# Re-placing four pieces of work in an attention and expert kernel: the maxima by couples, the late weight splits, gelu's table, and the last tokens' halves

## The reference, cut to what matters

```python
x = x + attention(layernorm(x), ctx)      # 8 heads of 64, softmax over the 1601 context rows
x = x + ffn(layernorm(x))                 # 1024 tokens

# attention: q = x Wq, k = ctx Wk, v = ctx Wv; softmax(q k^T / 8) v; then Wo and bo
# ffn: h = gelu(x w1 + b1) for a shared expert and for 8 experts,
#      expert_out = h w2 + b2, weighted by the router's two largest softmax probabilities,
#      plus the shared expert's output
```

## Time and profile before

| | us |
|---|---|
| median of 3 runs | 410.04 |
| profiled execution | 411.02 |
| its span, first to last instruction | 409.1 |
| PE busy | 399.1 (98%) |
| DVE busy | 284.6 (70%) |
| ACT busy | 247.9 (61%) |
| POOL busy | 237.0 (58%) |

### The profile page before, as it was taken

One profiled execution on the slowest core, in us unless ns is written; L12 is line 12 of the kernel. 1 busy time (PEld: TensorE's weight loads), 2 busy tenths in 40 slices (PEclk: granted clock), 3 DMA queues, 4 the chain that ended last, 5 costly groups with the idle time before them and its releaser, 6 DMA issues.

```text
span 409.1 us, 9721 instructions
## 1 busy us (share of the span) xinstructions
PE 399.1 (98%) x3718; PEld 333.0 (81%) x3718; DVE 284.6 (70%) x580; ACT 247.9 (61%) x399; POOL 237.0 (58%) x167
## 2 busy tenths in 40 slices
PE   8999999999999999999999999999999989999996
PEld 7787979798878887978788879797888777768886
DVE  4977788797537787976368778775586844566644
ACT  5677557383856472828555637287354554797882
POOL 7437668785804874729038756371183950687881
PEclk9999999999999999999999999999999989999999
DMA  6600002000000020000000300000000021102300
GB/s 202 186 3 0 2 2 63 2 3 2 2 0 2 2 62 3 2 2 3 0 2 3 117 3 2 2 0 2 2 3 2 3 102 50 56 0 93 135 8 27
DMA packets 17141, 11.77 MB, mean 29 GB/s; under 512 B 10188, under 2 KB 14136, under 8 KB 17096
## 3 DMA queue, kind: packets, MB, share of 16 engines
q1 hardware_dynamic: 17096, 11.15, 10.0%
HBM read 10.55 MB, written 0.56 MB: 27 GB/s over the span
## 4 chain that ended last, share of the span: by engine, by line
PE 87%; issue 3%; ACT 3%; POOL 3%; DVE 2%; DMA 1%; SPq 1%; ACTq 0%; DVEq 0%; POOLq 0%
PE ps L1189 21%; PE ps L1173 16%; PE ps L1020 10%; PE ps L1022 10%; PE ps L1021 10%; PE ps L1114 8%; PE ps L1164 6%; PE ps L1060 2%; PE ps L1121 2%; PE ps L1052 2%; ACT probs L797 1%; POOL work L483 1%; DMA probs<-in_L_xattn_Wv_dram 1%; ACT ps L822 1%; POOL kq_lo L699 1%
## 5 line engine op out<-in xcount | busy, mean ns | idle before, releaser
L915 DVE TENSOR_REDUCE maxes<-ps 128x1 f32<-128x402 f32 x256 | 132.5, 570 | 14.5 <-PE ps L1114 10.0
L797 ACT ACTIVATE probs<-ps 128x1024 f32<-128x1024 f32 (+1 forms) x112 | 105.6, 962 | 30.4 <-PE ps L1173 27.4
L483 POOL TENSOR_TENSOR work<-work,probs 128x1024 f32<-128x1024 f32 x45 | 107.4, 2387 | 3.5
L481 POOL TENSOR_TENSOR work<-probs 128x1024 f32<-128x1024 f32 x15 | 36.0, 2399 | 105.0 <-issue 89.3
L1189 PE MATMUL ps<-probs,v_sb 128*64 128x256 f32 (+1 forms) x832 | 93.4, 381 | 0.4 <-DVE work L858 0.4
L1189 PEld LDWEIGHTS ps<-probs,v_sb 128*64 128x64 f32 (+1 forms) x832 | 59.2, 137 | 30.7 <-issue 3.4
L1173 PE MATMUL ps<-kq_hi,kq_lo 64*128 64x256 f32 (+1 forms) x416 | 70.3, 282 | 0.0
L1173 PE MATMUL ps<-kq_lo,kq_hi 64*128 64x256 f32 (+1 forms) x416 | 70.2, 281 | 0.0
L1173 PE MATMUL ps<-kq_hi 64*128 64x256 f32 (+1 forms) x416 | 70.2, 281 | 0.0
L753 ACT COPY repeated<-rden 128x256 f32<-128x256 f32 x16 | 6.5, 404 | 93.0 <-DVE rden L894 93.0
L1114 PE MATMUL ps<-kq_hi 64*128 64x402 f32 x256 | 60.1, 366 | 0.1
(11 more groups left out here) (151 smaller groups left out, 698.8 us busy)
## 6 DMA issues: line engine op xcount, KB each, us to landing
v_sb<-weight_rows SPq DMA_DIRECT2D x12, 256.0 KB, 4.1
raw<-in_ctx_T_dram SPq DMA_DIRECT2D x3, 600.4 KB, 5.4
work<-in_L_ffn_rw_dram SPq DMA_DIRECT2D x1, 1024.0 KB, 7.5
shift_rows<-neg_row SPq DMA_DIRECT2D x64, 0.5 KB, 2.0
raw<-weight_rows SPq DMA_DIRECT2D x4, 256.0 KB, 3.5
raw<-in_ctx_T_dram SPq DMA_DIRECT2D x3, 150.8 KB, 2.4
x_sb<-in_x_dram SPq DMA_DIRECT2D x1, 384.0 KB, 5.4
wo_sb<-in_L_xattn_Wo_dram SPq DMA_DIRECT2D x1, 256.0 KB, 6.0
```

The costliest lines, as they stand in the source:

```text
L483: ops.tensor_tensor(acc, acc, pr, ALU.add).then_inc(summed, 1)
L797: nc.scalar.activation(dst, src, ACT.Exp, scale=SCALE).then_inc(probs_ready, 1)
L915: v.tensor_reduce(maxes[:, p % 2, i * T + t, blk:blk + 1], src[:, 0:BW], AX.X, ALU.max).then_inc(ring_taken, 1)
```

## The change

Four things change.

1. Maxima. Two of the next pair's 16 maxima, not three, go in front of the first unit; then two follow behind each unit. Unit 5 is cut: its first chunk, two maxima, then its second chunk as a step of its own (`second_chunk`), which now raises `scores_ready`. The product's matmuls are the same ones, written in a function.
2. `w2_low`. Ahead of the first low part POOL waits until all additions of pair 14 are done, DVE's too (`added(B - 1, PAIRS - 2)`).
3. gelu's table. In the step `add` of pair 15, which in ACT's order is behind its last exp of attention, ACT does one gelu of 128 x 1 into an unused tile. The table load comes in front of it.
4. `xt` of the last batch. Its step moves from behind the weighing of the sixth expert turn to between its `first` and its `weigh`. PE's order stays as it was; on DVE the two halves come before two weighings and not after them.

```diff
     for n, (b, p) in enumerate(order):
         ahead = maxima[n + 1] if n + 1 < n_order else []
-        out += ahead[:3]
+        out += ahead[:2]
         for u in range(n_units):
             out.append(("scores", (b, p, u)))
-            out += ahead[2 * u + 3:2 * u + 5]
+            out += ahead[2 * u + 2:2 * u + 4]
+            if u == n_units - 2:
+                out.append(("second_chunk", (b, p, u)))
...
-    amid = {0: [("spread", last_pair)], 1: [("ring", ("y", b))], 5: [("ring", ("xt", b))],
+    amid = {0: [("spread", last_pair)], 1: [("ring", ("y", b))],
             6: [("ring", ("router", last)), ("exp", last)]}
...
             out += [("first", i) for i in new]
+            if (h, turn) == (0, 5):
+                out.append(("ring", ("xt", b)))
             out += [("weigh", i) for i in new if e < experts]
...
                 if kind == "w2_low":
+                    if w == 0:
+                        added(B - 1, PAIRS - 2)
                     pool.wait_ge(w2_hi_ready, w + 1)
...
+                elif kind == "add" and w == LAST_PAIR:
+                    act.wait_ge(s_bias_turned, 1)
+                    nc.scalar.activation(turned[:], biasT[:, 0:1], ACT.Gelu)
...
+            def chunk_of_scores(b, p, u, j):
+
+                pair, c = b * PAIRS + p, UNITS[u][j]
+                banks = score_banks(unit_no(b, p, u))
+                rows = REST if u == NU - 1 else P
+                ks = slice(c * P, c * P + rows)
+                hi, lo = k_hi[:, pair % 2, ks], k_lo[:, pair % 2, ks]
+                factors = ((hi, q_hi[:, pair % 4, :]), (hi, q_lo[:, pair % 4, :]), (lo, q_hi[:, pair % 4, :]))
+                for i, (keys, queries) in enumerate(factors):
+                    for h in (1, 0):
+                        dims = slice(DH * h, DH * h + DH)
+                        ins = mm(banks[0:rows, h, j * S:(j + 1) * S], keys[dims], queries[dims], start=False,
+                                 stop=(i == len(factors) - 1 and c == UNITS[u][-1]))
+                return ins
...
-                    ins.then_inc(scores_ready, 1)
+                    for j in range(1 if u == NU - 2 else n_c):
+                        ins = chunk_of_scores(b, p, u, j)
+                    if u != NU - 2:
+                        ins.then_inc(scores_ready, 1)
+                elif kind == "second_chunk":
+                    chunk_of_scores(*w, 1).then_inc(scores_ready, 1)
```

More of the change, by code:

```diff
@@ L285, in build @@
         biasT = sb("biasT", [P, NE * HK])
+        turned = sb("turned", [P, 1])
         w1_sb = work[:].rearrange("p a b -> p (a b)")[:, 4 * PAIRS * S - NE * H:].rearrange("p (e h) -> p e h", e=NE)
```

## The result

The changed kernel took **405.81 us** (405.57 to 415.9, 4 runs) where the kernel before, run beside it, took 409.82 (408.36 to 410.78): a ratio of 0.9899, 95% interval 0.9865 to 0.9933. Faster, inside the range of 399.8 to 406.0, but 3.1 us above the forecast of 402.7 and outside its own range of 401.6 to 403.8. It lies where rival (b), couples that bring nothing, was put (404.5 to 407), and in what rival (d) was given (404.6 to 406.1); the experiments tell them apart.

What follows compares the result with a forecast made beforehand. TensorE, busy 98% of the span, was taken as the bound, so only its waits and clock count. Gains 1.7 + 3.0 + 0.6 + 2.0 = 7.3 us gave 403.7 profiled, 402.7 us median; own range 401.6 to 403.8, 8 in 10 399.8 to 406.0.

Steps and rivals of the forecast that it cites:

- rival (b): Scores stages: the couples of maxima bring nothing or lose, 1.7 becomes 0 to -3 us, time 404.5 to 407; chance 0.12.
- rival (d): Pair 15's additions, beside the splits, become late as pair 14's were: 404.6 to 406.1 us; chance 0.08.
- Couples, 1.7: Maxima in couples in 15 scores stages: 0.12 us gained per ordinary pair, 1.7 us in sum, bounds -5 to +6.
- the step in front of unit 5: Scores stage: paired maxima keep array halves in step, 1.18 us a unit instead of 1.24; unit 5 starts 0.4 us earlier.
- seams for nothing: Two matmuls in a row on the same array half, 14 places a pair, were taken to cost 0.
- the pairs with layernorm: Pairs 6, 10 and 14: unit 5 starts late anyway, so gains of 0.2, 0.2 and 0.3 us.
- The wait for the bank: Inside unit 5, the couple's second maximum waits 0.25 us for its PSUM bank.
- the balance of unit 5: Scores stage: 0.4 us gained against 0.43 delayed with 0.09 back, so unit 5's exp starts 0.1 us earlier.
- Late splits, 3.0: Around pairs 14 and 15: POOL held back ends the row-sum wait and clock fall, 2.8, plus 0.2 from earlier adds: 3.0 us.
- gelu's table, 0.6: Before the output projection: table load moved to idle ACT brings the chain 1.0 us sooner, 0.6 us gained, bounds 0 to 0.8.
- Tokens' halves, 2.0: At the router: wait gone, 1.0, clock fall gone, up to 1.7, 0.7 given back; net 2.0 us, 1.1 if it falls.
- From one execution to the median: Last term: the median of runs, 410.04, lies 0.98 us below the profiled 411.02, so 403.7 becomes 402.7 us.

## Why the forecast was right in sign and wrong in size

Step by step, from profiled execution to profiled execution (span 409.1 to 404.1, 5.0 us; the forecast's sum was 7.3):

- **Couples, 1.7: wrong, -0.4.** This is the step whose mechanism failed. Its parts held: the step in front of unit 5 (1.16 a unit against 1.18 forecast), seams for nothing, the bank back 1.0 us after its maximum's start, the pairs with layernorm (0.18, 0.20 and 0.24 against 0.2, 0.2 and 0.3). The wait for the bank was even shorter than said, 0.16 on PEld and not 0.25. What failed is the balance of unit 5. The forecast put 0.4 gained against 0.43 delayed with 0.09 back, so exp 0.1 earlier. Measured are 0.37 gained (6.19 to 5.82) and 0.45 lost: exp starts 188.54 - 186.86 = 1.68 us behind unit 5's shift row, where it was 187.76 - 186.53 = 1.23. So exp came 0.08 later. The rows show the stalled half out of step and "x2" not back before the end of the stage; that this is what takes the 0.09 that should have come back is read from them, not tested. PE met that exp in every ordinary pair: 0.12 gained became 0.04 lost, eleven times 0.16 or 1.8 us. Pair 0 lost 0.55 instead of 0.35. The four kernels with and without couples, and with and without the query projection first, show the cause rather than arguing it: with PE's wait for exp covered, thirteen pairs gain 1.96 us on the kernel before, and from pair 0 to pair 14's values it is 1.5 us more than with maxima as before, about the 1.7 that the forecast gave them.
- **Late splits, 3.0: right.** From pair 14's values (0.45 late) to pair 15's (2.57 early) 3.0 us. The wait is gone, the clock at 1.00. Undoing it alone shows 1.2 to 1.3 of it without a fall. Most of the rest is the fall that stood in before's profiled execution. Rival (d) did not come: of the four additions of pair 15 in one row (5.87 us, where before they took 5.01) two were slowed, by 0.4 each, and their sums were in time. The prediction was wrong, though, in reading the half microsecond that an addition lost as speaking against an exclusive lock; the last section shows that it fits one.
- **gelu's table, 0.6: right.** Load at 337.02 on an idle ACT, no idle time before the output projection (345.76 follows without a gap); undone alone, 0.7.
- **Tokens' halves, 2.0: right as a sum, wrong as a split.** The last two edits together gave 2.49 us (-2.57 to -5.06), 2.6 forecast. Of the halves' share the wait was meant to give 0.3 net and the clock 1.7, and that is what was measured with one fall against none. But a second wait, for the first half's output bank, was not in the working, and makes the net wait 0.0 to 0.3.
- **From one execution to the median: wrong by 1.0.** This term failed too. I subtracted 0.98, as if the changed kernel's executions would scatter round its profiled one as those of before did. But half of before's scatter is the falls of the clock that the change abolishes: its profiled execution had two, its median one or none. The 3.2 us of clock in the sum are worth, per execution of before, (26 + 2 x 8) / 64 x 1.4 = 0.9 us. The changed kernel has no fall to lose, so 403.7 and not 402.7 was what the sum said of it. 2.1 and 1.0 make the miss of 3.1. That 405.81 still lies inside the range is luck: its upper bound was 406.0, 0.2 us away, and two terms of the working had failed.

Put in medians without a fall the change gives 3.0, from 406.8 to 403.8. The other three edits together, without the couples, give 406.8 - 404.05, some 2.75; undone one by one they give 1.3 for the splits, 0.7 for the table and 0.3 for the halves, together 2.3. The 0.4 between these two stays open. So does the couples' own part: 0.4 lost in the traces, 0.2 gained by these medians, 0.6 gained by the medians of the kernel with maxima alone (406.15 without a fall). Executions of the changed kernel alone, none with a fall, have spans from 403.3 to 404.7, so these small differences settle nothing.

## What to carry to other kernels

When two engines meet at a bank at the end of every stage, a gain in the middle of the stage is only as large as what the last release moves: work out when that release comes, and before cutting into its path look for work of the waiting engine that doesn't need it and stands just behind (here one projection, 2.5 us for a swap of two list entries). A clock fall seen in one profile is one draw and not a term: count over several executions how often the mean clock shows it, and price it at that share. And don't move from a profiled execution to the median by before's own distance if the change removes what makes that distance.

## What was not expected of the hardware

- The same program and the same waits give no, one or two falls of the clock in 30, 26 and 8 of 64 executions. A wait of 1.35 us at pair 14's row sums was followed by one in at most 2 of 10, one of 1.0 us before the router's small matmuls in 6 of 11. The Trainium skill ("TensorE: Matmul & The Clock Gate", Part 1) says that the number of matmuls at the low clock at a kernel's start varies from run to run. What varies here is another thing: whether a fall comes at all in the middle of the kernel.
- GpSimd's splits and VectorE's additions take turns. In the kernel before, around the addition of 324.68:

```profile
324.60 0.72 POOL L678 TENSOR_TENSOR ctxT_hi<-raw,w_hi 128x256 fp32r<-128x256 f32 x1
325.28 1.71 POOL L678 TENSOR_TENSOR ctxT_hi<-raw,w_hi 128x256 fp32r<-128x256 f32 x1
326.44 1.11 DVE L485 TENSOR_TENSOR work<-work 128x512 f32<-128x512 f32 x1
326.96 1.17 POOL L678 TENSOR_TENSOR ctxT_hi<-raw,w_hi 128x256 fp32r<-128x256 f32 x1
327.58 1.09 DVE L486 TENSOR_TENSOR work<-work,probs 65x512 f32<-65x512 f32 x1
```

  They end one behind the other: a split at 325.32, the addition at 326.41, a split at 326.99, an addition at 327.55, a split at 328.13. The steps, 1.09, 0.58, 0.56 and 0.58, are each what the instruction takes alone (1.23, 0.72, 0.69 and 0.72) less 0.13 to 0.14. So an instruction that starts while the other engine's runs seems to wait until that one is through, but for a short part at its start. The addition of 324.68 had 325.32 - 324.68 = 0.64 to wait and lost 1.73 - 1.23 = 0.50. This is read from rows of two kernels (pair 15 of the changed one has the same steps); no run was made to test it.
